# First attention: row maxima as two 64-row products on the two halves of the array, in a two-layer network on Trainium2

## What is computed

```python
q = _apply_rope_subspace(q, DR)
k = _apply_rope_subspace(k, DR)
scale = 1.0 / np.sqrt(DH).astype(np.float32)
scores = jnp.einsum('bhqd,bhkd->bhqk', q, k) * scale
attn = jax.nn.softmax(scores, axis=-1)
out = jnp.einsum('bhqk,bhkd->bhqd', attn, v)
out = out.transpose(0, 2, 1, 3).reshape(b, s, H * DH)
out = out @ w_out.T + residual
```

## Time and profile before

| | |
|---|---|
| median of 3 runs | 2236.38 us (2236.3 to 2242.65) |
| the profiled execution, its own time | 2237.01 us |
| its span, first to last instruction | 2235.1 us |
| mean granted TensorE clock | 0.940 |
| first product of maxima, first score, last score | 46.0, 61.4, 1285.2 us |
| busy: PE, DVE, ACT, POOL | 2009.0, 1694.8, 1625.8, 1633.9 us |

### The profile page before, as it was taken

One profiled execution on the slowest core, in us unless ns is written; L12 is line 12 of the kernel. 1 busy time (PEld: TensorE's weight loads), 2 busy tenths in 40 slices (PEclk: granted clock), 3 DMA queues, 4 the chain that ended last, 5 costly groups with the idle time before them and its releaser, 6 DMA issues. The chain is left out here.

```text
span 2235.1 us, 60603 instructions
## 1 busy us (share of the span) xinstructions
PE 2009.0 (90%) x24318; PEld 1317.7 (59%) x24318; DVE 1694.8 (76%) x3487; ACT 1625.8 (73%) x3282; POOL 1633.9 (73%) x1036
## 2 busy tenths in 40 slices
PE   5899999999999999999999979976678787887888
PEld 2466666666666666666666646642456666666665
DVE  5677777777778777777777558978988898899624
ACT  3798898988988988988889936656656555574543
POOL 4799998999999999989989936626664334577700
PEclk8899999999999999999999989977889999899769
DMA  4000100010000001000100000111211111121201
GB/s 151 22 23 16 30 23 16 23 29 18 23 23 23 23 19 27 23 16 23 30 16 23 2 16 23 40 36 25 41 41 48 34 43 36 32 46 36 43 10 38
DMA packets 88224, 67.80 MB, mean 30 GB/s; under 512 B 41280, under 2 KB 78352, under 8 KB 87952
## 3 DMA queue, kind: packets, MB, share of 16 engines
q1 hardware_dynamic: 76432, 52.19, 9.1%
q0 software_dynamic: 11520, 11.82, 2.6%
HBM read 32.97 MB, written 1.61 MB: 15 GB/s over the span
## 5 line engine op out<-in xcount | busy, mean ns | idle before, releaser
L428 POOL TENSOR_TENSOR probs_lo<-probs,probs_hi 128x1024 f16<-128x1024 f32 x512 | 1077.0, 2134 | 87.3 <-ACT probs L477 86.2
L533 DVE TENSOR_REDUCE part_max<-aux 128x1 f32<-128x512 f32 x1024 | 690.0, 688 | 210.9 <-PE aux L608 206.0
L476 ACT ACTIVATE probs_hi<-scores 128x512 f16<-128x512 f32 x1024 | 632.8, 618 | 162.7 <-PE scores L641 149.0
L477 ACT ACTIVATE probs<-scores 128x512 f32<-128x512 f32 x1024 | 638.7, 624 | 0.0
L1732 POOL DMA_INDIRECT far<-key_table,placeT x320 | 328.6, 1027 | 236.8 <-issue 70.1
L655 PE MATMUL acc<-v,probs_hi 128*128 128x65 f16 x4096 | 445.9, 193 | 1.8 <-POOL probs_lo L428 1.8
L657 PE MATMUL acc<-v,probs_hi 128*128 128x64 f16 x4096 | 446.9, 195 | 0.0
L659 PE MATMUL acc<-v,probs_lo 128*128 128x65 f16 x4096 | 445.2, 193 | 0.0
L655 PEld LDWEIGHTS acc<-v,probs_hi 128*128 128x128 f16 x4096 | 383.0, 97 | 72.1 <-POOL probs_lo L428 2.1
L608 PE MATMUL aux<-k_a,q_a 128*128 128x512 f16 x1024 | 394.4, 386 | 32.4 <-issue 22.9
L657 PEld LDWEIGHTS acc<-v,probs_hi 128*128 128x128 f16 x4096 | 380.8, 97 | 68.9 <-issue 0.6
(11 more groups left out here) (335 smaller groups left out, 3619.1 us busy)
## 6 DMA issues: line engine op xcount, KB each, us to landing
q_a<-rope_high SPq DMA_DIRECT2D x128, 64.0 KB, 2.0
far<-key_table,placeT POOLq DMA_INDIRECT x360, 2.5
q_b<-rope_low SPq DMA_DIRECT2D x64, 64.0 KB, 2.0
k_b<-rope_high SPq DMA_DIRECT2D x64, 64.0 KB, 2.0
k_a<-rope_high SPq DMA_DIRECT2D x64, 64.0 KB, 2.1
k_a<-rope_low SPq DMA_DIRECT2D x64, 64.0 KB, 2.0
qT<-qT SPq DMA_DIRECT2D x16, 256.0 KB
queries<-places SPq DMA_DIRECT2D x7, 512.0 KB, 3.7
```

What stands on the lines that cost most here:

```text
L428: pool.tensor_tensor(probs_lo[:, slot], probs[:, wide], probs_hi[:, slot], ALU.subtract).then_inc(low_ready, 1)
L476: act.activation(probs_hi[:, slot, i], bank, ACT.Exp, scale=float(DH0) ** -0.5)
L477: act.activation(probs[:, wide, i], bank, ACT.Exp, scale=float(DH0) ** -0.5).then_inc(probs_ready, 1)
L533: dve.tensor_reduce(part_max[g % 2][:, n % QT, n // QT:n // QT + 1], bank, AX.X, ALU.max).then_inc(aux_free, 1)
```

## The change

The maximum is now taken of the high halves alone: the query's high half against the key's high half, 64 rows instead of 128. Two such products, of units `n - 1` and `n` (`n` odd: two query tiles against the same chunk of keys), are issued behind each other: the first with rows 0 to 63 of `q_a` and of `k_b`, the second with rows 64 to 127 of `q_a` and of `k_a`, each with 128 columns of weights, 512 streamed, and a PSUM bank of its own. Both units of a pair are due at the half step, and the pair goes out where its second unit stands. It waits for the bank of the unit three before its second, which means that of three banks two are free. The wait for the key's low halves moves from the maxima to a head's first score.

```diff
-            plan += [(KPAIR * g - 12.5 + n / 2, "max", (g, n)) for n in range(NCH * QT)]
+            plan += [(KPAIR * g - 12.5 + n // 2, "max", (g, n)) for n in range(NCH * QT)]
...
+                def two_maxima(g, n):
+
+                    u = unit_no["max", (g, n)]
+                    h, c = g // NCH, n // QT
+                    if u >= AUX:
+                        pe.wait_ge(aux_free, u - AUX + 1)
+                    if n == 1:
+                        wait_high(pe, rope_no["q", h, g % NCH // 2])
+                    if n % QT == 1:
+                        wait_high(pe, rope_no["k", h, c // 2])
+                    for m, keys in enumerate((kb[h % 2], ka[h % 2])):
+                        t, rows = (n - 1 + m) % QT, slice(m * LAT0, (m + 1) * LAT0)
+                        pe.matmul(aux[(u - 1 + m) % AUX][:], qa[g % QRING][rows, t * P:(t + 1) * P],
+                                  keys[rows, c * CH:(c + 1) * CH], start=True, stop=True).then_inc(aux_full, 1)
+
                 def fill(kind, arg):
 
+                    if kind == "max":
+                        if arg[1] % 2:
+                            two_maxima(*arg)
+                        return
...
-                    elif kind == "max":
-                        g, n = arg
-                        h, t, c = g // NCH, n % QT, n // QT
-                        if n == 0:
-                            wait_high(pe, rope_no["q", h, g % NCH // 2])
-                        if t == 0:
-                            wait_high(pe, rope_no["k", h, c // 2])
-                            wait_low(pe, rope_no["k", h, c // 2])
-                        ins = pe.matmul(bank, qa[g % QRING][:, t * P:(t + 1) * P], ka[h % 2][:, c * CH:(c + 1) * CH],
-                                        start=True, stop=True)
...
                         wait_low(pe, rope_no["q", h, g % NCH // 2])
+                        if n % STEPS == 0:
+                            for pair in range(PAIRS):
+                                wait_low(pe, rope_no["k", h, pair])
```

## The result

The changed kernel takes 2255.58 us (median of 5 runs, 2246.16 to 2257.13) where the kernel before takes 2239.46 beside it (5 runs): a ratio of 1.0059, interval 1.0038 to 1.0081. Run again in the study it gave 1.0043 (1.0023 to 1.0062). It is slower by about half a per cent; the forecast was no change, to within 0.3%.

What follows compares the result with a forecast made beforehand. PE's own sequence was taken to bound the kernel. Pairs -3.7, wait for the query's high halves -1.3 and start +1.7 gave -3.3 us on 2237.01, about 2233 us; range 2222 to 2280.

Steps and rivals of the forecast that it cites:

- the sentence on the banks: In the loop, the bank of the unit three before a pair's second was claimed emptied in time; nothing added.
- the sum: Pairs in the loop -3.7, wait for the query's high halves -1.3, kernel start +1.7: -3.3 us on 2237.01.
- The landing: Once per head PE waits for the query's high halves; this hides the way into the pair, 1.3 us saved.
- The pair: In the loop, a pair costs 0.4275 us for 0.435; 499 pairs save 3.7 us, bounds 11 saved and 3.7 lost.
- The start: Before the first score: high halves land 1.3 us earlier, but pairs take 1.40 us instead of 1.20; 1.7 lost.
- Halves one after the other: Rival, each pair: the second product starts 0.2175 us behind the first; 104 us more, 2337; chance 0.11.
- Weights that show: Rival, each pair: weight loads add up to 0.09 us, 45 us in all, 2278, half of it 2256; chance 0.10.
- A cheaper switch: Rival, each pair: only one array switch paid, 2188 us, or neither, about 2160; chance 0.09 together.
- the last part: Signs of error: second product 0.2 us late, step under 1.95, or PE waiting for DVE's banks over some us.

Runs made afterwards that it cites:

- the repeat: The changed kernel once more, with no edit: 2249.78 us (8 runs), ratio 1.0043 to the kernel before.
- with its ropes moved: The kernel before with both query ropes of each head due one step earlier (steps 14 and 27): 2218.02 us, ratio 0.9891.
- the run on the same rows: The changed kernel with both 64-row products of a pair on rows 0 to 63: 2359.24 us in one execution.
- the single halves: The kernel before with one 64-row product in place of each full maximum product, at the old due times: 2430.93 us in one execution.

## Why the prediction was wrong

**The step that failed** is the sentence on the banks: a rope bank "emptied before PE has done the 24 weighing products", and "I add nothing there". It took one rope bank for both. The first part's bank is free after one operation of DVE (L519); the second part's is held through two (L522, L527), in the example until 604.15, and the pair was ready at 603.62. Only where a shift stands between rope and pair is it the second part's bank that the pair needs, once a head: 15 x 0.59 = 8.9 us. The wait could have been read beforehand: the rows of DVE at that step of the profile before show L527 at 600.91, behind the maximum, and the change's wait for one unit more names it. In the terms of the sum, -3.7 - 1.3 + 1.7 = -3.3 us became 8.9 for the bank, 1.7 for the landing, 1.3 for the start (below) and -2.1 for all else: 9.7 us lost, beside 8.9 between the medians of the repeat. The 16.1 between the medians of the first five runs are 6.4 more; the changed kernel's five spread over 11.0, and why their median lies so high isn't shown.

**The landing** had the wrong sign. 14 x 0.09 = 1.3 us saved were forecast, as the way into the pair hides behind the wait. It does; but a maximum that had run ahead of the landing now stands behind it, and 15 x 0.11 = 1.7 us are lost. It was counted what the wait hides of the new work, not what it had hidden of the old.

**The pair** was right to a hundredth of a microsecond at each of its four places. Its gain in the sum was put too high: 3.7 us were forecast, and with the landing's wait gone for the most part the 15 heads at the upper clock are 1.3 us shorter with pairs (1112.63 and 1113.92), 2.7 without PE's idle time. The sum's own caveat, 0.015 us a pair either way, is wider than the difference.

**The start** was right in its mechanism. Timeline of PE and SP there:

```profile
40.63 0.60 SPq L407 DMA_DIRECT2D k_a<-rope_high  x1
...
42.84 0.58 PE L588 MATMUL aux<-k_b,q_a 64*128 64x512 f16 x1 [7.05 <-DMA k_a<-rope_high]
...
44.21 0.61 PE L588 MATMUL aux<-k_b,q_a 64*128 64x512 f16 x1 [0.75 <-DVE part_max L533]
```

1.37 us from the first pair to the second (the third starts at 45.60, 1.39 later) for the 1.40 forecast, and the first product 2.21 us behind the last high transfer's issue (2 us were taken). This execution issued that transfer 1.95 us earlier than the one before (40.63 and 42.58) and had its first score 0.7 earlier, so the start costs some 1.3 us of its own, near the 1.7 of the sum. It repeats: from that issue to the first score the kernel before takes 18.82 us, and 18.73 with its ropes moved, the changed one 20.07, and 20.02 once more.

**The rivals.** Halves one after the other: no, and the run on the same rows shows the price it would have had, 102 us of loop for the 104 worked out. Weights that show: no, 0.23 and not 0.22 behind the pair's first score is all. A cheaper switch: no; the single halves paid it every time. On the Trainium skill (TensorE: Matmul & The Clock Gate, Part 3): the trace agrees that products on different row groups start within hundredths of a microsecond (both at 695.85), and shows that their span is not the whole price between full-array products: 0.32 us to the next product and 0.13 ahead, not 0.22 and 0.03. None of the rivals was the case that came; a wait for DVE's banks was named only in the last part, as a sign that would make the prediction wrong, and had no price and no chance. The measured time lies inside the range, which the weights' rival had stretched, so the range held for another reason than the one given.

## What to carry to other kernels

When a change makes an instruction wait for one buffer more of a ring, write down for every kind of step which unit that buffer belongs to and when its last reader is done: one step of 32 decided this case. Where a product waits for a transfer, ask what ran ahead of the wait as well as what hides behind it. And a wait that both versions share can be worth more than the change: one due time moved by one step was worth over 20 us in either kernel, where the two shapes differ by one to three, less than the medians can tell.

## What the runs showed of the hardware

Two products of 64 rows by 128 columns on different rows start together and cost PE 0.21 us less than on the same rows (0.32 and 0.53 to the next product). A change of the array's shape costs 0.09 to 0.10 us each way, also for a single product in between (whether by the change itself or by a weight load that no longer runs ahead isn't shown), and the way from one column of weights (the shift) to 64 rows costs one such switch, not two. So shapes are worth grouping: one switch less in 63 steps took 7.1 us from the loop.
